# Seven chained products for `hid` from pair 1 on, one fixed order of events beside the Householder steps, and the identity added inside PSUM in the inverse

## What is computed

```python
h = maximum(layernorm(x), 0)                  # layer 0, W = adj * adj
h = relu(W @ (h @ W1)); h = relu(W @ (h @ W2)); x = x + W @ (h @ W3)
h = maximum(layernorm(x), 0)                  # layer 1
L_norm = D^-1/2 (diag(deg) - sym(adj)) D^-1/2; _, U = eigh(L_norm)
h = relu((U.T @ h) @ V1 + b1); x = x + U @ (h @ V2 + b2)
```

## Time and profile before

| what | value |
|---|---|
| median of 3 runs | 2251.55 us |
| profiled execution: its own time | 2251.1 us |
| profiled execution: span | 2249.4 us |
| steps (stage 1) end on PE at about | 1374.5 us |
| pairs 22 to 31 with Sturm counts (stage 2) | to about 1990 us |
| PE / DVE / ACT / POOL busy | 99 / 85 / 53 / 54% of the span |

### The profile page before, as it was taken

How to read it: one execution, slowest core, us unless ns; L and a number is a source line. 1 busy time by engine, 2 the same in 40 slices (tenths; PEclk the granted TensorE clock), 3 DMA queues, 4 the chain that set the end, 5 groups by cost and what they waited for, 6 DMA issues and landing times.

```text
span 2249.4 us, 47996 instructions
## 1 busy us (share of the span) xinstructions
PE 2223.1 (99%) x12694; PEld 1931.1 (86%) x12694; DVE 1909.5 (85%) x10565; ACT 1182.4 (53%) x2955; POOL 1224.2 (54%) x1956
## 2 busy tenths in 40 slices
PE   7999999999999999999999999999999999999999
PEld 6788888888888888888888887999999999899998
DVE  7999999888888888888777778969999998567776
ACT  5555555555555545555555554554555555345554
POOL 6555555544555555555555557664666666343332
PEclk9999999999999999999999999999999999999999
DMA  3000000000000000000000000000000001024443
GB/s 106 29 29 29 25 15 29 29 29 21 29 29 29 29 29 21 17 28 28 28 28 28 29 29 20 30 29 11 29 28 28 28 29 39 19 83 132 135 131 108
DMA packets 90031, 90.15 MB, mean 40 GB/s; under 512 B 5376, under 2 KB 89088, under 8 KB 89856
## 3 DMA queue, kind: packets, MB, share of 16 engines
q1 hardware_dynamic: 89856, 88.23, 12.3%
HBM read 54.66 MB, written 33.55 MB: 39 GB/s over the span
## 4 chain that ended last, share of the span: by engine, by line
PE 96%; DVE 2%; POOL 1%; ACT 1%; issue 1%; DMA 0%; SPq 0%; DVEq 0%; ACTq 0%; POOLq 0%
PE ps L1670 78%; PE ps L1865 10%; PE ps L1575 4%; PE ps L1875 1%; PE ps L1808 1%; DVE A L1066 0%; PE ps L1732 0%; PE ps L1689 0%; POOL w3sum L601 0%; DMA xl<-in_x_dram 0%; DVE prods L1103 0%; POOL hid2T L643 0%; PE ps L1762 0%; PE ps L1764 0%; PE ps L1763 0%
## 5 line engine op out<-in xcount | busy, mean ns | idle before, releaser
L557 POOL COPY Eb<-sc 128x1 f32<-128x1 f32 (+1 forms) x254 | 47.4, 187 | 434.0 <-DVE v L1155 219.5
L1670 PE MATMUL ps<-agg2T,w 128*128 128x256 f32 x1024 | 239.3, 379 | 0.0
L1670 PE MATMUL ps<-hid2T,xin 128*128 128x256 f32 x1024 | 236.3, 379 | 2.5 <-issue 2.5
L1670 PE MATMUL ps<-weightT,hid 128*128 128x256 f32 x1024 | 236.5, 379 | 0.7 <-ACT hid L959 0.7
L1670 PEld LDWEIGHTS ps<-weightT,hid 128*128 128x128 f32 x1024 | 189.5, 191 | 34.5 <-issue 10.0
L1670 PEld LDWEIGHTS ps<-hid2T,xin 128*128 128x128 f32 x1024 | 189.0, 190 | 28.0 <-issue 2.9
L1670 PEld LDWEIGHTS ps<-agg2T,w 128*128 128x128 f32 x1024 | 188.3, 190 | 25.4
L846 ACT ACTIVATE hid2T<-ps 128x512 f32<-128x512 f32 x256 | 151.2, 590 | 103.8 <-PE ps L1670 102.2
L1269 DVE SCALAR_TENSOR_TENSOR ahead<-ps,ne,ahead 128x14 f32<-128x14 f32 (+1 forms) x1020 | 189.4, 227 | 0.0
L1266 DVE RECIPROCAL ps<-ahead 128x14 f32<-128x14 f32 (+1 forms) x1024 | 187.7, 229 | 0.1
L1670 PE MATMUL ps<-w,aggT 128*128 128x512 f32 (+1 forms) x424 | 179.4, 556 | 0.0
(11 more groups left out here) (403 smaller groups left out, 6264.7 us busy)
## 6 DMA issues: line engine op xcount, KB each, us to landing
xl<-in_x_dram SPq DMA_DIRECT2D x64, 256.0 KB, 2.9
xr<-in_x_dram SPq DMA_DIRECT2D x64, 256.0 KB, 2.9
x_dram<-xr SPq DMA_DIRECT2D x64, 256.0 KB, 2.3
xin<-x_dram SPq DMA_DIRECT2D x64, 256.0 KB, 2.8
out_dram<-xin SPq DMA_DIRECT2D x64, 256.0 KB, 2.3
w<-in_L_gnn_W_dram SPq DMA_DIRECT2D x1, 2048.0 KB, 10.5
w<-in_L_gnn_W_dram SPq DMA_DIRECT2D x1, 1024.0 KB, 12.3
w<-in_L_gnn_W_dram SPq DMA_DIRECT2D x1, 512.0 KB, 5.8
```

The lines of the kernel that those rows point to most:

```text
L557: pool.tensor_copy(Eb[:, bass.ds(k, 1)], sc[:, 4:5])
L1670: ins = pe.matmul(dst, a, b, start=start, stop=stop, skip_group_check=plan_.units[i][0][0] in "HPG")
```

## The change

- **`GROUPS`, `FIRST_LATE = 1`:** pair 0 keeps `FULL`. Pairs 1 to 21 get `LATE`, so that all later `hid` are seven products. The plain `hid` of pair 1 (`first_hid`) is dealt over the first steps of pair 1 (`BRIDGE`), and L1732's at pair 22 goes. The group (12, 21) is split into (12, 13) and (13, 21).
- **Order:** from pair 1 on ACT follows one list (`ACT_ORDER`) and POOL another (`SUMS_ORDER`). `late_placed` cuts both into steps by a model of start times: an event of ACT stands in the step in which the model starts it, behind that step's `step_root`. In pairs 2 to 10 this puts the evacuation of the third unit, `agg2`(0,1), behind the root of the second step; P1(0) writes the same bank and its first matmul stands four matmuls (of `agg2`(1,0)) behind `step_x` of that step. In the pairs from 1 on the last step holds, on POOL, `hid`1, `hid`2 and the two `add_x`, and on ACT `hidfin`2 last. From `beside` with the new parts, 12-step pairs have one transpose and four 256-column matmuls behind `step_q` in their 6th and 12th step, where it was five.
- **Sums of W1** move on POOL from behind the last step into the first two steps of pair 1.
- **Inverse:** `cross` first writes the identity into both halves of its PSUM bank with one 256-column matmul and adds onto it; `join` then needs one product for each quarter, and its four matmuls with `eye` a level go. The sign moves from the copy of `Gn` to that of `gramV`.

```diff
         GROUPS = [(n, n + 1, 11, 0.54) for n in range(11)]
-        GROUPS += [(11, 12, 12, 0.54), (12, 21, 12, 0.54), (21, 22, 13, 0.54)]
+        GROUPS += [(11, 12, 12, 0.54), (12, 13, 12, 0.54), (13, 21, 12, 0.54), (21, 22, 13, 0.54)]
...
         PAIRS = B // 2
+        FIRST_LATE = 1
...
@@ -294,13 +295,25 @@
 
             if plan_ is FULL:
                 return PERIOD * pair + 2
-            return LATE_PERIOD * pair + (PERIOD - LATE_PERIOD) * WITH_STEPS + 2 + len(LATE_HID)
-
-        def beside(steps, share):
+            return LATE_PERIOD * pair + (PERIOD - LATE_PERIOD) * FIRST_LATE + 2 + len(LATE_HID)
+
+        def plan_of(pair):
+
+            return LATE if pair >= FIRST_LATE else FULL
+
+        LATE_WORK = [(i, m, 1 if st[0] == "G" else 2) for i, (st, _, _) in enumerate(LATE.units)
+                     for m in range(2 if st[0] == "H" else 4)]
+        BRIDGE = [(n - len(LATE_HID), m, 4) for n in range(len(LATE_HID)) for m in range(FB)]
+
+        def work_of(pair):
+
+            return WORK if pair < FIRST_LATE else BRIDGE * (pair == FIRST_LATE) + LATE_WORK
+
+        def beside(steps, share, parts):
 
             filled = [([], []) for _ in range(steps)]
-            total, done = sum(size for _, _, size in WORK), 0
-            for i, m, size in WORK:
+            total, done = sum(size for _, _, size in parts), 0
+            for i, m, size in parts:
                 step, place = divmod(done * steps / total, 1)
                 filled[int(step)][int(place >= share)].append((i, m))
                 done += size
...
+        LN_AFTER = {0: [(0, 0)], 1: [(0, 1)], 3: [(1, 0)], 4: [(1, 1)], 6: [(2, 0)], 11: [(2, 1)]}
+        FINS_AFTER = {8: [0], 9: [1], 10: [2], 11: [3], 12: [4], 13: [5]}
+        HID_AFTER = {LATE.at["res", 0, 0]: 0, LATE.at["res", 1, 0]: 1, LATE.at["H4", 0, 0]: 2}
+
+        ACT_ORDER = []
+        for i in range(LATE_PERIOD):
+            ACT_ORDER += [("evac", i)] + [("ln",) + x for x in LN_AFTER.get(i - LATE_P, [])]
+            ACT_ORDER += [("fin", n) for n in FINS_AFTER.get(i - LATE_P, [])] + [("hidfin", HID_AFTER[n]) for n in (i,) if n in HID_AFTER]
+        SUMS_ORDER = [("turn", n) for n in range(1, 5)] + [(kind, j) for kind in ("mean", "scale") for j in range(2)]
+        SUMS_ORDER += LATE_ORDER + [("x", j) for j in range(2)]
+
+        def late_needs(event, bridge):
+
+            kind, n, at = event[0], event[1], LATE.at
+            if kind == "unit":
+                stage, j, q = LATE.units[n] if n >= 0 else ("first", 0, 0)
+                if n < 0:
+                    return []
+                out = [("evac", emptied(LATE, n))] if emptied(LATE, n) >= 0 else []
+                if stage == "agg2" and bridge:
+                    out += [("evac", 2 * j - 3)]
+                if stage == "agg":
+                    out += [("ln", 2, j)]
...
+            if kind in ("fin", "hidfin"):
+                return [("add" if kind == "fin" else "hid", n)]
+            if kind == "ln":
+                return [[], [("mean", event[2])], [("scale", event[2])]][n]
...
+        def late_placed(steps, share, bridge):
+
...
+                start, engine = min(ready)
+                event = lines[engine].pop(0)
+                kind, n = event[:2]
+                took = size[n] * 62.0 / total if kind == "unit" else TOOK.get(kind, 0.65 if kind == "evac" else 1.35)
+                if kind == "evac" and n >= 0 and LATE.units[n][0][0] == "G":
+                    took = 0.35
+                began[event], ended[event] = start, start + took
+                free[engine] = start + took
+                behind = [slots[x] for x in late_needs(event, bridge) if x in slots]
+                if kind == "unit":
+                    assert all(x <= first[n] for x in behind), (event, steps)
+                    slots[event] = last[n]
+                else:
+                    wanted = int((start if engine == "act" else max(start - 3.2, 0)) // tau)
+                    slots[event] = max(behind + [min(wanted, steps - 1)])
...
+        def slots_of(pair, steps, share):
+
+            return placed(steps, share) if pair < FIRST_LATE else late_placed(steps, share, pair == FIRST_LATE)
...
+                elif kind == "mean":
+                    ln_minus_mean(pair + 1, n)
+                elif kind == "scale":
+                    ln_scale(pair + 1, n)
+                elif kind == "x":
+                    add_x(pair, n, plan_)
...
+                    if isinstance(t, int) and t == FIRST_LATE and s < 2:
+                        pool.wait_ge(load_w1, 16)
+                        for n in range(2 * s + 1, 2 * s + 3):
+                            sum_of_w1(n)
...
             for k in TAIL:
                 keep_reflector(k, NB - 1)
-            pool.wait_ge(load_w1, 16)
-            for n in range(1, 5):
-                sum_of_w1(n)
 
             pool.memset(halves[:, :, :], 0.0).then_inc(halved, 1)
...
+            def evacuate_first(n):
+                j, q = LATE_HID[n]
+                act.wait_ge(unit, before(FIRST_LATE) + n + 1)
+                act.activation(hid[:, j, q, :], ring[n][:, :], ACT.Relu).then_inc(evac, 1)
+
+            def event(pair, plan_, kind, n, j=0):
+                if kind == "evac" and n < 0:
+                    evacuate_first(n + len(LATE_HID))
+                elif kind == "evac":
+                    evacuate(pair, n, plan_)
+                elif kind == "ln":
+                    LN[n](pair + 1, j)
+                elif kind == "hidfin":
+                    finish_hid(pair + 1, n)
                 else:
                     finish(pair, n)
...
             act.wait_ge(gram_v, 1)
-            act.activation(gramV[:, :, :].rearrange("p a n -> p (a n)"), ps[3][:, 0:2 * P], ACT.Copy)
+            act.activation(gramV[:, :, :].rearrange("p a n -> p (a n)"), ps[3][:, 0:2 * P], ACT.Copy, scale=-1.0)
             act.activation(VT[:, :, :].rearrange("p a n -> p (a n)"), ps[2][:, 0:3 * P],
...
                 if n < 2 * TREE and n % 2 == 0:
-                    ins = act.activation(Gn[:, :, :].rearrange("p a n -> p (a n)"), ps[0][:, 0:2 * P],
-                                         ACT.Copy, scale=-1.0)
+                    ins = act.activation(Gn[:, :, :].rearrange("p a n -> p (a n)"), ps[0][:, 0:2 * P], ACT.Copy)
                 elif n < 2 * TREE:
...
-            link(dve.tensor_scalar(dg[:, 0:2], dg[:, 0:2], 0.5, 1e-36, ALU.mult, ALU.max))
+            link(dve.tensor_scalar(dg[:, 0:2], dg[:, 0:2], -0.5, 1e-36, ALU.mult, ALU.max))
...
-                    from_hid = isinstance(pair, int) and pair == WITH_STEPS and emptied(plan_, i) < 0
+                    from_hid = isinstance(pair, int) and pair == FIRST_LATE and emptied(plan_, i) < 0
...
+            def first_hid(n, m):
+
+                j, q = LATE_HID[n]
+                if m == 0:
+                    pe.wait_ge(evac, before(FIRST_LATE) + n - 4 + 3)
+                ins = pe.matmul(ring[n][:, :], aggT[:, j, m, P * q:P * q + P], w1[:, m, :], start=m == 0, stop=m == FB - 1)
+                if m == FB - 1:
+                    ins.then_inc(unit, 1)
+
+            def part_of(pair, i, m, plan_):
+                if i < 0:
+                    first_hid(i + len(LATE_HID), m)
+                else:
+                    work(pair, i, m, m + 1, plan_)
+
...
-            for n, (j, q) in enumerate(LATE_HID):
-                pe.wait_ge(evac, before(WITH_STEPS) + n - 4 + 3)
-                for dst, a, b, start, stop in group(ring[n][:, :], [(aggT[:, j, f, P * q:P * q + P], w1[:, f, :]) for f in range(FB)]):
-                    ins = pe.matmul(dst, a, b, start=start, stop=stop)
-                ins.then_inc(unit, 1)
             for i in range(LATE_PERIOD):
...
+                pe.matmul(ps[0][:, 0:2 * P], eye, ident[:, 0, 0:P].unsqueeze(1).to_broadcast([P, 2, P]),
+                          start=True, stop=False, skip_group_check=True)
                 for a in range(2):
                     ins = pe.matmul(ps[0][:, P * a:P * a + P], crossed[:, l, a, :], Tt[:, 0, a, :],
-                                    start=True, stop=True)
+                                    start=False, stop=True, skip_group_check=True)
                 ins.then_inc(t_made, 1)
 
             def join(l):
                 pe.wait_ge(t_saved, 2 * l + 1)
                 for a in range(2):
                     upper, lower = ps[1][:, P * a:P * a + P], ps[1][:, N + P * a:N + P * a + P]
-                    pe.matmul(upper, eye, Tt[:, 0, a, :], start=True, stop=False)
-                    pe.matmul(upper, Tt[:, 1, a, :], Gn[:, a, :], start=False, stop=True)
-                    pe.matmul(lower, eye, Tt[:, 1, a, :], start=True, stop=False)
-                    ins = pe.matmul(lower, Gn[:, a, :], Tt[:, 1, a, :], start=False, stop=True)
+                    pe.matmul(upper, Tt[:, 1, a, :], Gn[:, a, :], start=True, stop=True)
+                    ins = pe.matmul(lower, Gn[:, a, :], Tt[:, 1, a, :], start=True, stop=True)
```

(59 more changed lines are left out.)

82 lines of the change are left out of this document (48 added, 34 removed).

## The result

The changed kernel took **2244.33 us**, median of 7 runs (2242.99 to 2244.8), beside 2251.5 for seven runs of the kernel before (2250.37 to 2252.12). The ratio is 0.9968, 95% interval 0.9958 to 0.9978: faster by 0.32%, more than the 0.2% that can be told from no change. The forecast was 2243.3.

A forecast was written before the change was run, and what follows sets the result against it. PE, busy 99% of the span, was taken as the bound: steps -5.5, their end -2.2, clock +2.7 and inverse -3.25 gave -8.25, a profiled 2242.85 and a median of 2243.3 us, range 2235 to 2248.

The forecast's parts named there:

- 3d: DVE's half-steps where the new dealing leaves one matmul fewer, and some tenths behind 3a: +1.4, bounds 0 and 4.0.
- Term 1: PE work beside the steps: 30 pairs with seven products instead of plain `hid`, 0.82 less a pair; -10.3 in the steps.
- Terms 2 and 3: Waits in the steps: those of the old order go, -4.0; those of the new order come in four places, +8.8.
- 3a: P1(0), pairs 2 to 10: PE waits for the copy of `agg2`(0,1) behind the second step's root; +4.2, bounds 0 and 5.0.
- 3c: First `step_q` of one-block pairs: the root starts late behind `hidfin`2, which follows POOL's sums; +1.9.
- Term 4: Where the steps end: POOL's queue sets P5's start, W1's sums leave it, a longer last step takes some back; -2.2.
- Term 5: P5 after the steps: a PE wait of 8.3 us drops its clock to half speed; +2.7, bounds 0 and 3.5.
- Rival C: PE's clock holds through the wait at P5: 2240.6, counted within the forecast's own spread of chance 0.74.
- Term 6: The inverse, where PE is the bound: 28 `eye` matmuls go and seven of 256 columns come; -3.25.
- Rivals A and B: A: the new order waits nowhere, 2235.8, chance 0.13. B: PE's arithmetic alone, all waits go, 2223.7, chance 0.01.
- D: Slower: the root behind `hidfin`2 is late by a whole sum (1.25) in all 21 pairs; +26, 2269, chance 0.04.
- E: No change that can be told: terms 3 and 4 at their worse ends, slower clock recovery; -1.7, 2249.9, chance 0.08.

The follow-up runs named there:

- experiment 5: Changed kernel with `hidfin`2 of pairs 2 to 20 moved behind the first root of the next pair's first step; 2240.94 us.
- experiment 3: Changed kernel with POOL's crossed products and `T` put behind the turns that P5 waits for, in pair 22 alone; 2233.78 us.
- experiment 1: Changed kernel with each ACT copy out of PSUM placed in the step in which its unit ends; 2239.63 us.
- experiment 6: Changed kernel with pairs 1 to 10 keeping the plain `hid` and old order, seven products only after pair 11 (FIRST_LATE = 11); 2250.19 us.
- experiment 2: Changed kernel with 18 unused matmuls on PE ahead of P5 in pair 22, where it would idle; 2241.94 us.
- experiment 4: Kernel before the change with only the inverse changed: identity added inside PSUM, no `eye` copies in the joins, sign moved; 2248.31 us beside 2251.51.
- experiment 7: Changed kernel with three edits together: copies in the step where the unit ends, turns first in pair 22, third relu behind the next root; 2226.14 us.

## Why the prediction was right

The mechanism was right in each of its six terms, but for one place of waits that it had not seen (under 3d); the sizes were right in most of them.

- **Term 1, PE work, -10.3: right.** The counts came as worked out, and pair 10 lasts 62.32 with 0.11 of waiting before and 61.65 with 0.27 after: 0.83 less of work, 0.82 forecast.
- **Terms 2 and 3, waits, +4.8 forecast, +6.7 counted (+6.4 by the times): the term that was mis-sized.** Of term 2, 4.4 went where 4.0 was forecast. 3a was forecast at 4.2 from 0.65 down to 0.25; measured .67 .63 .59 .54 .50 .42 .33 .27 .25, which is 4.2. 3b: 1.3, measured 1.33. 3c: 1.9, measured 1.6 at `step_q` of pairs 11 to 21, and its cause shown by experiment 5. The failed one is 3d, "the small ones": 1.4 forecast, about 4 measured, at its upper bound. 1.2 are transposes late in pairs 11 to 21 (they wait for DVE's `col`, with one matmul fewer ahead of them), 1.2 are transposes and `step_q` of pairs 2 to 5, and 1.6 stand at a place that I had not seen at all: the first matmuls behind a pair's first two transposes in pairs 11 to 21, up to 0.33 a pair (none before). In pair 14 the transpose starts at 892.11 and the next matmul at 892.40, where a pitch of 0.11 is due, and the one behind it is 0.10 late as well. Those behind the first transpose stand almost all (1.1 of 1.2) in pairs 13 to 20, which the kernel runs as one `pe.Fori` loop; pairs 10, 11 and 21, unrolled, have none. In the loop PE's sequencer computes the numbers that it waits for by register instructions. In pair 14 they end at 892.34, right ahead of the weight load at 892.39, while the relu and the copy that the unit waits for had ended at 889.79 and, at the latest, 891.99. So in pair 14 it is not ACT's work that PE waits for. That the sequencer holds it fits, but no run takes this away, and the loop of the old order (pairs 12 to 20) shows no such wait.
- **The steps: -5.5 forecast, -3.9 measured.** That is the excess of the waits, 1.9 as counted, less 0.3 outside of them.
- **Term 4, end of the steps, -2.2 forecast, -1.3 measured.** It was POOL's queue, as said, and experiment 3 shows it. The memset starts 3.6 after the last passes of the steps (3.1 forecast, 5.3 before), and from there to the turn it takes 17.8 instead of 17.4; why those 0.4 came I don't know. The wait at P5 was 8.66 of idleness, forecast 8.3.
- **Term 5, clock, +2.7 forecast, +3.1 measured** in this execution, 1.5 to 3.1 in four executions of kernels with the same wait (experiments 1, 5, 6). Rival C, that the clock holds, is refuted by the granted 0.50 in the trace after, and its price by experiment 2. One premise was wrong: from the end of the kernel I took it that PE falls within some 2.5 us of idleness, and at P5 the clock held for 4.5 us of it. The wait was long enough all the same. The Trainium skill, "TensorE: Matmul & The Clock Gate", section "HAM oscillation — how this bites in real kernels", says that a group of matmuls behind an idle wait starts at half clock; the trace after agrees with 10.19 for 32 passes. In experiment 4 the group started at full clock and lost it 0.8 us later.
- **Term 6, the inverse, -3.25 forecast, -3.2 measured** alone (experiment 4), and -3.0 in the profile after, the 3.1 of clock left out. The cover at the root of pair 30 shrank by 2.3 and not by 3.25; why stays open.
- **Start-up, not in the forecast: -1.3** in the profiled pair. Without it the sum would be -5.1 against a forecast of -8.25. The time was met to 1.0 us, then, partly because chance at the start went the right way; the median of seven runs (-7.2) holds less of it than one profile does, but I can't say how much. The clock may have helped too: the profiled execution of the kernel before lost nothing behind its wait at P5, but the 16 executions of it beside experiments 1 to 4 took 2250.06 to 2250.63 (6 of them) or 2251.35 to 2252.33 (10), and a loss like the 1.8 of experiment 4 in the ten would fit. Then the median before holds a part of term 5 already. No trace of the ten was kept, so this stays open.

Rivals A and B fell with the waits at P1 and the 8.66 at P5. D fell: the root is late behind the relu by 0.1 to 0.2 us of PE time a pair, not by 1.25. E came nearest on the other side: its waits (12 forecast, 11.1 measured) were almost there.

## What to carry to other kernels

When work is taken off a bound engine, look at each in-order queue that releases it next: a copy that stands behind a later step's short but dependent instruction (ACT's root here) cost PE 0.25 to 0.67 us a pair in nine pairs, where the seven products had given 0.82. Products that nobody needs for 100 us (the crossed ones, made at 1379.42, are first used at 1504) should not stand ahead of the one sum that the bound engine waits for; this one order was worth 10.6 us, more than the whole change. And an idle wait of PE has a second price behind it, its clock, which the run with unused matmuls in its place showed to be 3 us in the trace and 2.4 by the medians.

## What the runs showed of the hardware

- A wait of 2.5 us on PE cost no clock in one execution (2.52, clock 1.00) and cost 1.8 us in another (2.48, experiment 4: granted 1.00 through the wait and for 0.8 us of work behind it, then 0.50 for 3.3 us). So an idle time of this length isn't safe, and one profile doesn't tell.
- What a spell at half clock costs differs from run to run. The first 16 passes of the aggregates take 3.62 at full clock; the executions profiled took 6.34, 5.02, 5.66, 4.74, 5.66, 4.90, 5.07 and 4.87 (before, after, experiments 1 to 5 and 7), which moves the start of the steps between 17.50 and 18.97. Behind the same 8.5 to 8.7 us of idleness, the 32 passes of P5 took 10.19, 9.27, 8.56 and 9.56 (after, experiments 1, 5 and 6) for 7.07. Together that is enough for the spreads of some 2 us between runs of one kernel, and it bounds what one pair of profiles can tell.
- PE's matmuls behind the first transpose of a one-block pair start up to 0.28 late in sum in the new order (pair 14), and neither the copies at home nor the turns first changed that; with the relu moved it is 0.18. They stand in the looped pairs 13 to 20, behind register instructions of PE's sequencer; what holds the rest was not isolated.
